# Group norms of an attention block with fewer one-column VectorE operations, and a shared reciprocal root with one operation less

## The reference

```python
x = _L0_conv_ref(x, ..., 8)               # group norm (8 groups), qkv, 8 heads of softmax attention over 1024 positions, projection, + x
x = x + _L1_conv_ref(_gn(x), ...)         # group norm (32 groups), depthwise convolutions, 1x1 convolution
t = _to_tokens(x)
t = t + _L2_attn_ref(_ln_t(t), ...)       # layer norm, attention through 16 landmarks
t = t + _L2_ffn_ref(_ln_t(t), ...)        # layer norm, 8 gelu experts, the best 2 of each token
t = t + _L3_attn_ref(_ln_t(t), ...)       # layer norm, attention
t = t + _L3_ffn_ref(_ln_t(t), ...)        # layer norm, 16 silu experts, the best 6, and shared ones
```

## Time and profile before

| what | us |
|---|---|
| median of 3 runs | 5571.4 (5562.84 to 5574.16) |
| span of the profiled execution, first to last instruction | 5548.6 |
| busy, PE / DVE / ACT / POOL | 4842.2 / 3586.2 / 2987.7 / 1021.9 |
| mean granted PE clock | 0.952 of full |

### The profile page before, as it was taken

One profiled execution on the slowest core, in us unless ns is written; L12 is line 12 of the kernel. 1 busy time (PEld: TensorE's weight loads), 2 busy tenths in 40 slices (PEclk: granted clock), 3 DMA queues, 4 the chain that ended last, 5 costly groups with the idle time before them and its releaser, 6 DMA issues.

```text
span 5548.6 us, 81822 instructions
## 1 busy us (share of the span) xinstructions
PE 4842.2 (87%) x25633; PEld 2616.5 (47%) x25633; DVE 3586.2 (65%) x7699; ACT 2987.7 (54%) x5420; POOL 1021.9 (18%) x1348
## 2 busy tenths in 40 slices
PE   5888888888888886957888888888899999999999
PEld 1222222222222221336777877787755555555554
DVE  6677777777777762555665656555576676766765
ACT  2655565665655653414555555556755455455552
POOL 2212112121222112202333333333210000000000
PEclk7999999999999998979999999999999999999999
DMA  2522222222222211223545454544321111111112
GB/s 84 144 70 81 81 70 70 70 73 78 73 89 82 66 45 38 29 68 106 165 140 163 141 162 147 157 146 129 106 61 45 50 48 45 50 46 47 52 45 75
DMA packets 406297, 477.10 MB, mean 86 GB/s; under 512 B 87640, under 2 KB 249648, under 8 KB 403760
## 3 DMA queue, kind: packets, MB, share of 16 engines
q1 hardware_dynamic: 372128, 424.84, 25.4%
q0 software_dynamic: 20576, 35.55, 2.3%
q10 hardware_dynamic: 13168, 11.48, 0.8%
HBM read 308.54 MB, written 145.57 MB: 82 GB/s over the span
## 4 chain that ended last, share of the span: by engine, by line
PE 33%; DVE 15%; issue 3%; DVEq 3%; ACT 2%; ACTq 0%; SPq 0%; DMA 0%
PE n_ps_f L2153 4%; PE n_ps_f L2146 4%; PE n_ps_xy L1801 3%; PE n_ps_h L1791 3%; PE n_ps_c L2193 2%; PE n_ps_h L2205 2%; PE n_ps_f L2140 2%; PE n_ps_f L1649 2%; PE n_ps_xy L2209 1%; DVEq L2025 1%; DVE n_stats L971 1%; DVE n_xln L983 1%; PE n_ps_f L995 1%; PE n_ps_h L2209 1%; DVE n_down_weights L2024 1%
## 5 line engine op out<-in xcount | busy, mean ns | idle before, releaser
L597 ACT ACTIVATE a_probs<-ps_b 128x512 f32<-128x512 f32 x2048 | 1111.0, 594 | 794.8 <-PE ps_b L693 782.0
L454 DVE TENSOR_REDUCE a_negmax<-ps_a 128x1 f32<-128x1024 f32 x1024 | 1206.1, 1219 | 378.9 <-PE ps_a L637 369.3
L637 PE MATMUL ps_a<-a_k_stack,a_q_stack 96*128 96x512 bf16 x2048 | 634.6, 396 | 178.8 <-DVE a_negmax L454 89.9
L693 PE MATMUL ps_b<-a_q_stack,a_k_stack 99*128 99x512 bf16 x2048 | 673.6, 391 | 68.2 <-ACT a_probs L597 30.9
L1604 ACT ACTIVATE n_hidden<-n_ps_h,n_b 128x128 f32<-128x128 f32 x1472 | 420.2, 374 | 339.1 <-PE n_ps_h L1791 338.3
L706 PE MATMUL ps_o<-a_probs,a_v_ones 128*32 128x512 f32 x4096 | 562.0, 622 | 0.2 <-ACT a_probs L597 0.2
L637 PEld LDWEIGHTS ps_a<-a_k_stack,a_q_stack 96*128 96x128 bf16 x2048 | 146.1, 99 | 732.2 <-DVE a_negmax L454 468.9
L1801 PE MATMUL n_ps_xy<-n_down_weights,n_hidden 128*128 x2944 | 410.7, 284 | 78.9 <-ACT n_xy L1618 72.8
L693 PEld LDWEIGHTS ps_b<-a_q_stack,a_k_stack 99*128 99x128 bf16 x2048 | 196.2, 100 | 487.8 <-ACT a_probs L597 251.5
L1801 PEld LDWEIGHTS n_ps_xy<-n_down_weights,n_hidden 128*128 128x128 f32 x2944 | 369.1, 196 | 117.0 <-issue 112.8
L1791 PE MATMUL n_ps_h<-n_xy,n_up_weights 128*128 128x128 f32 x2944 | 399.8, 279 | 3.6 <-issue 1.8
(11 more groups left out here) (346 smaller groups left out, 7532.8 us busy)
## 6 DMA issues: line engine op xcount, KB each, us to landing
n_up_weights<-in_L_ffn_W_dram SPq DMA_DIRECT2D x368, 256.0 KB, 2.7
n_up_weights<-score_scratch SPq DMA_DIRECT2D x512, 128.0 KB, 2.9
split_scratch<-a_pieces SPq DMA_DIRECT2D x180, 256.0 KB
a_q_stack<-split_scratch SPq DMA_DIRECT2D x128, 192.0 KB, 3.7
a_k_stack<-split_scratch SPq DMA_DIRECT2D x128, 192.0 KB, 4.1
rows_scratch<-n_zero SPq DMA_DIRECT2D x16, 1472.0 KB, 10.5
outs_scratch<-n_xy SPq DMA_DIRECT2D x176, 128.0 KB, 1.9
n_xg<-rows_scratch SPq DMA_DIRECT2D x80, 256.0 KB
```

Source lines behind the costliest of these rows:

```text
L454: dve.tensor_reduce(negmax[:, b, t:t + 1], bank, axis=AX.X, op=ALU.max, negate=True).then_inc(ring_read, 1)
L597: act.activation(probs[:, m % PROBS, 512 * k:512 * k + 512], ps_b[:, k, :], ACT.Exp).then_inc(b_exp, 1)
L637: last = pe.matmul(bank[:, cols], q_stack[0:KS, h, 128 * t:128 * t + 128], k_stack[0:KS, h, cols], start=True, stop=True)
L693: pe.matmul(ps_b[:, k, :], k_stack[:, h, 128 * t:128 * t + 128], q_stack[:, h, 512 * k:512 * k + 512], start=True, stop=True).then_inc(b_u ...
```

## The change

The helper `rsqrt` loses its operation L60: `v` stays as it is, and the factor -0.5 goes into the middle operation of each Newton step, which becomes a scalar_tensor_tensor with a constant. `rsqrt` is still called by `token_norm_steps`. A second helper, `rsqrt_column`, for one column only, has a Newton step of two operations: the first reads -0.5 * v as a scalar that is itself a column of SBUF. `group_affine` becomes `group_scale`, which makes that -0.5 * v on the way and leaves the shift out. For the first norm the shift is computed once, as mean * scale - norm_b, and subtracted at the end. For the second norm scale and shift are written to `gn2` at once and read from there.

```diff
--- before.py
+++ after.py
@@ -56,17 +56,26 @@
 def rsqrt(dve, y, v, t):
 
     dve.tensor_scalar(y.bitcast(I32), v.bitcast(I32), -0.5, 1597463007.0, ALU.mult, ALU.add)
-    dve.drain()
-    dve.tensor_scalar(v, v, -0.5, None, ALU.mult)
     for _ in range(3):
         dve.drain()
         dve.tensor_tensor(t, y, y, ALU.mult)
         dve.drain()
-        dve.tensor_tensor(t, t, v, ALU.mult)
+        dve.scalar_tensor_tensor(t, t, -0.5, v, ALU.mult, ALU.mult)
         dve.drain()
         last = dve.scalar_tensor_tensor(y, t, 1.5, y, ALU.add, ALU.mult)
     dve.drain()
     return last
+
+
+def rsqrt_column(dve, out, y, minus_half, t):
+
+    dve.tensor_scalar(y.bitcast(I32), minus_half.bitcast(I32), -0.5, 519526879.0, ALU.mult, ALU.add)
+    dve.drain()
+    for n in range(3):
+        dve.scalar_tensor_tensor(t, y, minus_half, y, ALU.mult, ALU.mult)
+        dve.drain()
+        dve.scalar_tensor_tensor(out if n == 2 else y, t, 1.5, y, ALU.add, ALU.mult)
+        dve.drain()
 
 
 def channel_moments(dve, moments, stats, mv, x):
@@ -80,19 +89,17 @@
     return dve.scalar_tensor_tensor(moments[:, 1:2], mv[:, 0:1], mv[:, 0:1], mv[:, 1:2], ALU.mult, ALU.add)
 
 
-def group_affine(dve, scale, shift, group, sums, sums_read, width, small, eps):
+def group_scale(dve, scale, group, sums, sums_read, width, small, eps):
 
     dve.tensor_scalar(group[:, :], sums, 1.0 / width, None, ALU.mult).then_inc(sums_read, 1)
     dve.drain()
-    dve.tensor_tensor(small[:, 0:1], group[:, 0:1], group[:, 0:1], ALU.mult)
+    dve.scalar_tensor_tensor(small[:, 0:1], group[:, 0:1], 0.5, group[:, 0:1], ALU.mult, ALU.mult)
     dve.drain()
-    dve.tensor_tensor(small[:, 1:2], group[:, 1:2], small[:, 0:1], ALU.subtract)
+    dve.scalar_tensor_tensor(small[:, 1:2], group[:, 1:2], -0.5, small[:, 0:1], ALU.mult, ALU.add)
     dve.drain()
-    dve.tensor_scalar(small[:, 1:2], small[:, 1:2], 0.0, eps, ALU.max, ALU.add)
+    dve.tensor_scalar(small[:, 1:2], small[:, 1:2], 0.0, -0.5 * eps, ALU.min, ALU.add)
     dve.drain()
-    rsqrt(dve, scale, small[:, 1:2], small[:, 2:3])
-    dve.scalar_tensor_tensor(shift, group[:, 0:1], -1.0, scale, ALU.mult, ALU.mult)
-    dve.drain()
+    rsqrt_column(dve, scale, small[:, 0:1], small[:, 1:2], small[:, 2:3])
 
 
 def attention_phase(nc, sems, handles, B, io, const, const_in, band_dram, u_cols, gn2, x1_dram, split_dram, sums_dram, conv):
@@ -475,11 +482,13 @@
                     channel_moments(dve, moments, stats, mv, x1).then_inc(moments2_up, 1)
                 elif what == "sums":
                     width, eps = ((C // 8, 1e-5), (C // 32, 1e-5))[work[1]]
-                    group_affine(dve, gscale[:, :], gshift[:, :], group, bank[:, 0:2], ring_read, width, small, eps)
+                    scale = gn2[:, 0, prev:prev + 1] if work[1] else gscale[:, :]
+                    group_scale(dve, scale, group, bank[:, 0:2], ring_read, width, small, eps)
                 elif what == "norm2":
-                    dve.tensor_copy(gn2[:, 0, bass.ds(prev, 1)], gscale[:, :])
-                    dve.tensor_copy(gn2[:, 1, bass.ds(prev, 1)], gshift[:, :])
-                    dve.tensor_scalar(xn[:, :], x1[:, :], gscale[:, :], gshift[:, :], ALU.mult, ALU.add)
+                    scale, shift = gn2[:, 0, prev:prev + 1], gn2[:, 1, prev:prev + 1]
+                    dve.scalar_tensor_tensor(shift, group[:, 0:1], -1.0, scale, ALU.mult, ALU.mult)
+                    dve.drain()
+                    dve.tensor_scalar(xn[:, :], x1[:, :], scale, shift, ALU.mult, ALU.add)
                     dve.drain()
                 elif what == "turn2":
                     dve.transpose(u_tr[:, :, :].rearrange("p c h -> p h c"), xn[:, :]).then_inc(ut_up, 1)
@@ -489,11 +498,10 @@
                     channel_moments(dve, moments, stats, mv, xf).then_inc(moments_up, 1)
                 elif what == "norm":
                     dve.tensor_tensor(gscale[:, :], gscale[:, :], nw[:, :], ALU.mult)
-                    dve.tensor_tensor(gshift[:, :], gshift[:, :], nw[:, :], ALU.mult)
                     dve.drain()
-                    dve.tensor_tensor(gshift[:, :], gshift[:, :], nb[:, :], ALU.add)
+                    dve.scalar_tensor_tensor(gshift[:, :], group[:, 0:1], gscale[:, :], nb[:, :], ALU.mult, ALU.subtract)
                     dve.drain()
-                    dve.tensor_scalar(xn[:, :], xf[:, :], gscale[:, :], gshift[:, :], ALU.mult, ALU.add).then_inc(xn_up, 1)
+                    dve.tensor_scalar(xn[:, :], xf[:, :], gscale[:, :], gshift[:, :], ALU.mult, ALU.subtract).then_inc(xn_up, 1)
                     dve.drain().then_inc(xf_free, 1)
                 elif what == "split":
                     dve.wait_ge(full_up, 2)
```

## The result

| | median | lowest to highest | runs |
|---|---|---|---|
| before, on the same chip | 5567.1 us | 5561.4 to 5574.2 | 4 |
| after | 5526.6 us | 5521.1 to 5534.2 | 4 |

The same kernel again in another set of runs: 5531.0 us, ratio 0.9941 (0.9927 to 0.9955), 33 us less. So the gain is 33 to 40 us. The new kernel's profiled execution took 5521.1 us with a span of 5519.3: only 1.8 us lie outside a span.

What follows compares the result with a forecast made beforehand. Neither PE nor VectorE was full; short norm strings cost only where somebody waits. Terms 1.0 + 0.9 + 8.7 + 14.2 = 24.8 us, nine tenths taken as 22, gave 5549 us from 5571.4, range 5536 to 5564.

Steps and rivals of the forecast that it cites:

- The eleven late maxima: Attention block: in eleven images the first row maximum comes late after the first norm; the shorter norm saves 8.7 us.
- next-profile part: Signs expected in the new profile: attention block ends 10 us sooner, token block 14 us shorter.
- Only the later blocks pay: Rival, 0.15: the attention block's eleven gains are given back in the same image; 16 us saved, 5555 us.
- The clock gives more: Rival, 0.10: q matmuls run before the clock falls in half of eleven images; 10 us on top, 5539 us.
- The 22.8 us kept outside the span: Whole kernel: the median of the runs stays 22.8 us above the profiled span, so 5526.6 becomes 5549 us.
- Layer norms: Token block: removing L60 with its drain saves 0.245 us at 58 places on the chain, 14.2 us.
- Layer norms hidden: Rival, 0.12: VectorE's expert work hides half or all of the token block's 14.2 us; about 5558 us, 5561 at the end.
- First norm and its price: Attention block: five drained steps go, column scalars cost 0.05 us each; net 1.0 us shorter per first norm.
- Second norms: Attention block: each 0.9 us shorter (0.8 to 1.3), worth something only in the last image, nothing inside the block.
- The nine tenths: Whole sum: 22 of 24.8 us taken, since somewhere in 71 places the second latest follows closer than the saving.
- The clock takes: Rival, 0.04: moved idle times make the clock fall on other matmuls, 1.8 us each; 5583 us and up.
- It does not do what its name says: Rival, 0.04: the chain misleads in both the attention and token blocks, so no effect; 5569 us.

Runs made afterwards that it cites:

- e6: Changed kernel with four drained one-column copies, which nothing reads, added in the second group norm of each image; 5533.4 us, 0.9951 of the kernel before.
- e5: Changed kernel with five drained one-column copies, which nothing reads, added in the first group norm of each image; 5548.2 us, 0.9976 of the kernel before.
- e4: Changed kernel, itself unaltered, timed and profiled a second time; 5531.0 us, 0.9941 of the kernel before.
- e8: Changed kernel with two Newton steps in place of three in the dense part's 32 layer norms; 5502.5 us, 0.9900 of the kernel before.

## Why the prediction was wrong

- **The eleven late maxima: the step that failed.** The forecast came out at 10.6 us for the block (10 in the next-profile part), 8.7 of them for the late maxima, because it priced the shorter string as a wait and put what the clock does behind it at nothing in the sum. That part is as forecast in kind: ten of the eleven start in time and the eleventh is 0.05 us late, and the wait fell by 7.1 us in the first pair (12.9 to 5.8; 6.0 in the means) for the 8.7. Nothing was given back later in the image, so the rival "Only the later blocks pay" is out. But the block gave 25 us by the times and 36 by the traces: in these, 17 of idle time, of which 8 are waits for the stacks' DMAs that stood in the sum at nothing, and 19 of PE's busy time with the same matmuls. I had the second as the rival "The clock gives more", at 0.10 and 10 us, for L663 alone and by fewer falls. The runs showed neither: in the first pair the q matmuls of fifteen images shortened from 52.6 to 48.3 us, 4.3 of the 10.8 us of busy time, and the rest lies in other matmuls; and the clock falls about as often but stays low half as long. If every microsecond at the low level costs half of one, the records of the granted clock (276 us low in the mean of the three old traces, 231 in the five new) put 22 or 23 us down to the clock and some 14 to the rest, and 14 is near my 10.6.
- **The 22.8 us kept outside the span: wrong.** A run has 1.8 us outside its span (1.75 to 1.85) in each of the thirteen profiled executions that have a time of their own. The span of 5548.6 belonged to one of the shorter executions (about 5550.4 us) of a kernel whose runs go from 5545 to 5575. The distance was luck in the clock, not a fixed cost. It did little to the forecast gain, since it was added to both sides, but it hid that one trace of the attention block can be off by 18 us.
- **Layer norms: inside the range, and shown by half.** 14.2 us forecast; 15 (8 to 21) measured on the kernel before, and 8 on top of the new group norms. The waits behind them shrank as counted (3.9 us in 16 places). The dense part is 7.2 us shorter (mean of 1700.1 in three traces with the old helper, 1692.9 in six with the new one), half of 14.2, but only 1.7 of that is idle time of PE (121.0 to 119.3): 5.5 are busy time, which the forecast had not in it. The gelu part shows its half in idle time only (224.7 to 220.0 in the means of three each) and is no shorter as a whole (1458.1 and 1457.3 in the same traces): its busy time goes from 1228 to 1246 us between traces of equal work, more than the 7 looked for. The rival "Layer norms hidden" named half or none of the 14.2; half of it is not excluded.
- **First norm and its price: right.** 0.96 us for the 1.0 forecast. The column scalar costs 0.060, not 0.05: (5 x 0.24) - (4 x 0.06) = 0.96. L75 and L77 are different operations, and no run exchanged the scalar alone; L96, which has a constant, takes 252 ns, for a reason that no run shows. The formula of the Trainium skill, VectorE: DVE Perf Modes, section on the TRN2 errata, (N + 151) / 0.96 ns for an fp32 tensor_tensor, puts one column at an estimated 158 ns; the trace agrees for L77 (159) and not for L75 (219).
- **Second norms: right.** Inside the block they cost nothing that could be measured (e6); at its end 1.19 us were won for 0.9, inside the bounds of 0.8 to 1.3.
- **The nine tenths: not decided.** I took off 2.8 us (24.8 - 22) for a second latest close behind. That is less than any interval here can tell; the total came out above the full sum, for the reason given above.
- **"The clock takes": not seen.** Every kernel with a part of the change was faster than before. "It does not do what its name says" is out as well: the first stage gave more than half.

What is shown: the length of the first norm sets the attention block's gain, and waits, and how long the clock stays low, move with it and back (e5). What is only argued: that the clock comes back sooner because the q matmuls wait less. In the old traces it also stays low for 6.8 us at 6 of 11 places where the q matmuls do not wait at all, with the maximum late all the same. The fill kept the clock up but moved the scores too, and I did not find which idle time decides a fall. The Trainium skill, TensorE: Matmul & The Clock Gate, section on how HAM oscillation bites in real kernels, describes a throttle that falls anew at each wait of a loop whose work between waits is shorter than the wait, so that its cost is paid once per turn. The traces agree that it is paid once per turn: without the fill the q matmuls take between 2.3 and 3.8 us in every image of the kernel before, with it 1.98. They do not agree on the condition: here the idle times ahead of the scores are 1.3 to 2.6 us, with some 60 us of work between them.

## What to carry to other kernels

Where PE waits for a string of small VectorE operations once per turn of a loop, price the wait, and then name what its clock does behind it as a term of its own, by how long it stays low and not only by how often it falls: here 6 us less of one wait came with 25 us by the times and 36 by the traces. Take two or three traces of the kernel before pricing anything by one, and cut them at the same instruction. Hunt the drained one-column operations first: each takes about 0.24 us of a wait that it stands in, and with two Newton steps everywhere the kernel had its lowest median, at the price of a coarser root.

## What the runs showed that I had not expected

- The same matmuls of the attention block took between 1814 and 1839 us of PE's time, by how long the clock was low. The spread of a kernel's runs goes with it: of the kernel before, the run of 5545.3 us had a mean granted clock of 0.954, that of 5575.4 us one of 0.949.
- An operation with a scalar read from a column took VectorE 0.060 us more at 128x1 than one with a constant (219 against 159 ns, 96 and 64 operations).
- Shortening the gelu part's strings by 20 us took 24 to 42 us off PE's busy time besides (against the traces of e5 and e4); doing the same in the dense part, where the clock was at 0.98, took only 3 to 8 us off it (1571.5 to 1575.7 in six traces, 1568.1 in e8).
- Filler matmuls lifted the attention block's clock from 0.94 to 0.97 in the kernel before and took 0.28% off its time (1 - 0.9972); on the changed kernel they won nothing.
